# One block of products with ones per attention group: softmax sums gathered by a third adding transfer in rotating buffers, with loads, division and copies moved in their orders

## The chip, the cores and the metric

The kernel runs on one core of a Trainium2 chip. The metric is the device time of one execution in microseconds (us), lower is better. Engines are named as in the profile: PE (TensorE), DVE (VectorE), ACT (ScalarE), POOL (GpSimd), SP (SyncE, which only issues transfers here).

## The reference

A gated cross-attention block on x (2 x 512 x 1024) with a context (2 x 1024 x 1024): a quantised product with the context, a LoRA layer, a grouped-query attention, and a mixture of experts. Each is scaled by a gate and added to x. The part that the change touches is the attention:

```python
q = (query @ Wq).reshape(b, sq, NUM_HEADS, HEAD_DIM).transpose(0, 2, 1, 3)      # 32 heads of 32
k = (key @ Wk).reshape(b, sk, NUM_KV_HEADS, HEAD_DIM).transpose(0, 2, 1, 3)     # 8 heads of 32
v = (value @ Wv).reshape(b, sk, NUM_KV_HEADS, HEAD_DIM).transpose(0, 2, 1, 3)
k = jnp.repeat(k, rep, axis=1); v = jnp.repeat(v, rep, axis=1)                  # rep = 4
scores = jnp.einsum('bhqd,bhkd->bhqk', q, k) * scale
probs = jax.nn.softmax(scores, axis=-1)
out = jnp.einsum('bhqk,bhkd->bhqd', probs, v)
```

with 512 queries and 1024 keys in each of two batches.

## The kernel before

Every engine runs a list of instructions written out by hand; semaphores join them. The attention is 16 groups (`GROUPS`: 2 batches x 8 key heads). A group is the four query heads of one key head, in 32 steps (`STEPS`): step t = 4*kt + h takes block kt of 128 keys and head h. The loop is `group(g)` on PE and `exp_group(g)` on ACT.

In a step PE issues one product for the maxima of a group that comes 52 steps later (`score_step`, bf16, 512 columns; DVE reduces it in `maximum`), and one transposed product of scores (L1046), which ACT turns into exponentials (L1401) in a ring of four probability tiles `PB`, each 128 x 2048 fp32 (four heads of 512 queries). Every four steps, in `weigh`, PE multiplies a finished tile by the values: four fp32 products of 32 columns of weights each that stand side by side in the array (one block). At step 16 the next group's maxima are turned (`max_rows`), DVE and SP bring them as rows to the keys and queries (`rows_in`), and PE waits for these at the next group's step 0.

The softmax sums over 1024 keys are gathered on POOL. For pair j of a group (tiles 2j and 2j+1, four pairs) POOL adds two tiles into a buffer (L668); ACT may reuse the two tiles only when that is done (`p_add`). The buffers are `PS[0]` and `PS[1]` (halves of R[4]) and `PS[2]` (`stage_pair`). Pairs 0 and 2 go into `PS[0]` and `PS[2]`, pairs 1 and 3 both into `PS[1]`; after each of the latter POOL starts an adding transfer (L671, 1 MB, SBUF to SBUF) of `PS[1]` onto `PS[0]` or `PS[2]`. PE multiplies both results by ones (`total(g, j)`, another block of four fp32 products each, summed over partitions into bank 6), at steps 2 and 18 of the next group (`TOTAL_AT`). ACT copies the sums out at step 20 (`SUM_OUT_AT`).

The reciprocals go a long way: SP spreads the sums over partitions (`sums_in`, four loads), DVE inverts at step 8 (`FEW_AT`, `invert_few`), SP writes 8 KB to memory and reads it back as broadcasts (`reciprocals_in`), POOL multiplies (`divide`, behind pair 1), ACT makes the upper half at step 28 (`O_HI_AT`, `divided_hi`) and POOL the lower (`divided_lo`, behind pair 2), all for the group before the last.

SP's order in group g is: rows of the maxima, sums of g-2, then (from the end of group g-1 on) queries and keys of g+2, then the reciprocals. PE needs these queries and keys at step 12 of group g. POOL's order in group g is: pair 0, the copy of the next values (`stage_values`), pair 1, transfer, division of g-2, pair 2, lower part, pair 3, transfer.

After the last step PE runs the output products (L1003) of one tile, the two blocks with ones of the last group, and the other tiles, of which the first products already stand in the last groups' steps.

## Time and profile before

| what | value |
|---|---|
| median of 3 runs | 1241.37 us (1240.68 to 1242.19) |
| the profiled execution | 1243.45 us, its span 1241.6 us |
| granted PE clock | 0.994 of full speed |
| attention stage in the span | 424 to 822 us |
| adding transfers | 32 of 1 MB |
| blocks with values / with ones | 128 / 32 |

The span is the time between the first and the last instruction of the profile; durations below are from this one execution. L668 is line 668 of the kernel. PE's matmuls are pipelined, so the distance between two beginnings says more than the length of one. A block of four products is shown as x8, since each fp32 product has two records. "[0.77 <-DMA stage_pair<-R]" is idle time of the engine before the instruction and what ended it.

### The profile page before, as it was taken

The numbers are of one execution on the slowest core, as the hardware profiler recorded it, in microseconds if no ns is written. First come the engines' busy times: TensorE is split into PE (matmuls) and PEld (weight loads), VectorE is DVE, ScalarE is ACT, GpSimd is POOL, SyncE is SP. The second block draws the span as 40 slices with busy tenths as digits, with TensorE's granted clock in tenths as the row PEclk, the third lists the DMA queues.
The fourth block names the chain that finished last, engine by engine and source line by source line (L and its number), as shares of the span: only waits on it lengthen the run. The fifth ranks groups of instructions, "written<-read, shape, count | busy, mean of one in ns | idle before, by whom it ended". The sixth has DMA issues, their size and how long they took to land.

```text
span 1241.6 us, 16902 instructions
## 1 busy us (share of the span) xinstructions
PE 1215.0 (98%) x6440; PEld 511.5 (41%) x6440; DVE 784.4 (63%) x1375; ACT 475.2 (38%) x829; POOL 685.1 (55%) x300
## 2 busy tenths in 40 slices
PE   8998899999999999999999999999999999999998
PEld 6664444444444332222323223234444444444443
DVE  8997731433546788887878788135659846737622
ACT  4676321000100377776777677743252010010000
POOL 6006996600072188988999899870175543535510
PEclk9999899999999999999999999999999999999999
DMA  9577242411361146564655455443374442523301
GB/s 353 176 252 187 68 126 79 102 35 35 62 207 60 35 92 129 114 131 105 129 118 126 108 120 110 99 90 60 101 215 138 132 136 102 176 79 103 118 17 51
DMA packets 94301, 145.11 MB, mean 117 GB/s; under 512 B 54672, under 2 KB 64912, under 8 KB 90128
## 3 DMA queue, kind: packets, MB, share of 16 engines
q1 hardware_dynamic: 59712, 99.51, 26.0%
q0 software_dynamic: 4608, 33.56, 13.5%
q10 hardware_dynamic: 29904, 11.02, 4.0%
q8 instruction: 48, 0.79, 0.2%
q14 instruction: 29, 0.24, 0.1%
HBM read 89.16 MB, written 10.60 MB: 80 GB/s over the span
## 4 chain that ended last, share of the span: by engine, by line
PE 54%; POOL 19%; DMA 14%; DVE 9%; issue 3%; ACT 1%; SPq 0%; POOLq 0%; ACTq 0%; DVEq 0%
PE bank L702 47%; POOL R L668 12%; DMA stage_pair<-R 9%; DMA R<-R 4%; PE bank L1003 4%; POOL stage_pair L668 4%; DVE R L1502 1%; POOL xn L650 1%; POOL R L690 1%; PE bank L958 1%; DVE R L1549 1%; DVE stats L1515 1%; DVE xn L1542 1%; DVE XTl L1549 1%; POOL XTl L655 1%
## 5 line engine op out<-in xcount | busy, mean ns | idle before, releaser
L1774 DVE TENSOR_REDUCE mxp<-bank 128x1 f32<-128x512 f32 x512 | 323.2, 683 | 87.0 <-PE bank L958 85.1
L1401 ACT ACTIVATE R<-bank 128x512 f32<-128x512 f32 x512 | 271.8, 602 | 108.7 <-PE bank L1046 102.8
L702 PE MATMUL bank<-XTh,R 128*128 128x512 bf16 x896 | 278.5, 379 | 2.7 <-POOL R L690 1.5
L668 POOL TENSOR_TENSOR R<-R 128x2048 f32<-128x2048 f32 x48 | 222.3, 4632 | 79.2 <-ACT R L1401 51.0
L702 PE MATMUL bank<-R 128*128 128x512 bf16 x960 | 209.2, 379 | 0.0
L702 PE MATMUL bank<-XTl,R 128*128 128x512 bf16 x448 | 169.6, 379 | 0.0
L690 POOL TENSOR_TENSOR R<-stage_pair,R 128x1024 bf16<-128x1024 f32 x32 | 76.5, 2403 | 129.6 <-DVE R L1932 69.1
L702 PEld LDWEIGHTS bank<-R 128*128 128x128 bf16 x960 | 94.0, 98 | 113.2
L971 PE MATMUL bank<-R,stage_c 128*32 128x512 f32 x1024 | 136.4, 604 | 0.5 <-ACT R L1401 0.5
L1046 PE MATMUL bank<-R 98*128 98x512 bf16 x352 | 133.9, 381 | 0.9 <-DVE R L1802 0.8
L958 PE MATMUL bank<-R 96*128 96x512 bf16 x352 | 134.4, 382 | 0.0
L702 PEld LDWEIGHTS bank<-XTh,R 128*128 128x128 bf16 x896 | 87.5, 98 | 105.9 <-POOL R L690 2.1
L690 POOL TENSOR_TENSOR R<-stage_c,R 128x1024 bf16<-128x1024 f32 x32 | 76.3, 2396 | 59.1 <-DVE R L1932 50.2
L1474 ACT ACTIVATE R<-bank,b1t 128x512 f32<-128x512 f32 x32 | 22.0, 686 | 201.9 <-PE bank L702 201.9
L573 POOL TENSOR_TENSOR R<-stage_pair,zero 128x1024 f32 (+1 forms) x35 | 67.2, 1921 | 37.7 <-DMA stage_pair<-wts_in 26.2
L575 POOL TENSOR_TENSOR R<-stage_pair,R 128x1024 f32 (+1 forms) x35 | 75.9, 2167 | 5.9 <-POOL R L573 5.3
L668 POOL TENSOR_TENSOR stage_pair<-R 128x2048 f32<-128x2048 f32 x16 | 76.5, 4783 | 0.9 <-ACT R L1401 0.8
L958 PEld LDWEIGHTS bank<-R 96*128 96x128 bf16 x352 | 34.2, 97 | 98.5 <-DVE mxp L1774 64.4
L1003 PE MATMUL bank<-R,XTh 128*128 128x512 bf16 x256 | 70.5, 379 | 0.8 <-issue 0.8
L1981 DVE SCALAR_TENSOR_TENSOR X<-xn,TV,X 128x512 f32<-128x512 f32 x32 | 67.4, 2146 | 0.1
L1199 ACT ACTIVATE lnv<-lnv 128x1 f32<-128x1 f32 x32 | 6.4, 201 | 156.8 <-DVE lnv L1522 156.8
L1962 DVE CAST R<-R 128x512 bf16<-128x512 f32 x32 | 21.3, 667 | 70.5 <-ACT R L1474 70.5
(201 smaller groups left out, 1504.8 us busy)
## 6 DMA issues: line engine op xcount, KB each, us to landing
stage_pair<-wts_in SPq DMA_DIRECT2D x35, 512.0 KB, 3.5
R<-R POOLq DMA_DIRECT2D x16, 1024.0 KB, 7.6
stage_pair<-R POOLq DMA_DIRECT2D x16, 1024.0 KB, 7.0
stage_pair<-w_in SPq DMA_DIRECT2D x32, 512.0 KB, 3.6
stage_c<-w_in SPq DMA_DIRECT2D x32, 512.0 KB, 3.6
R<-q_scr SPq DMA_DIRECT2D x48, 128.0 KB, 2.6
XTh<-ctx_t_in SPq DMA_DIRECT2D x11, 512.0 KB, 6.9
XTh<-ctx_nat_in SPq DMA_DIRECT2D x9, 512.0 KB, 3.6
```

Of the source, the lines that this page charges most:

```text
L573: pool.tensor_tensor(hi, stage_w[stage][:, :], zero[:, :].to_broadcast([P, D]), ALU.add).then_inc(wt_hi, 1)
L575: pool.tensor_tensor(lo, stage_w[stage][:, :], hi, ALU.subtract).then_inc(wt_done, 1)
L668: pool.tensor_tensor(PS[(0, 1, 2, 1)[j]], PB[2 * j % 4], PB[2 * j % 4 + 1], ALU.add).then_inc(p_add, 1)
L690: pool.tensor_tensor(lo[:, cols], stage_e[(n - N_WT) % RING_E][:, :], hi[:, cols], ALU.subtract).then_inc(wt_done, 1)
L702: mm = pe.matmul(o, a, m, start=first and a is ah and bs is bh, stop=last and a is al)
L958: pe.matmul(bank[s_bank(u)][:, :], QS[g % 3][0:96, h * S + qt * P:h * S + (qt + 1) * P], KS[g % 3][0:96, kh * HALF:(kh + 1) * HALF], start ...
L971: mm = pe.matmul(out_bank[h * HD:(h + 1) * HD, :], weights, probs[:, h * S:(h + 1) * S], start=first, stop=last)
L1003: mm = pe.matmul(outs[h], a[i][:, cols], b[i][:, k * D + h * HALF:k * D + (h + 1) * HALF], start=k == 0 and i == 0, stop=k == KT - 1 and i ...
L1046: pe.matmul(bank[t_bank(g, t)][:, :], KS[g % 3][0:98, kt * P:(kt + 1) * P], QS[g % 3][0:98, h * S:(h + 1) * S], start=True, stop=True).the ...
L1401: act.activation(PB[kt % 4][:, h * S:(h + 1) * S], bank[t_bank(g, t)][:, :], ACT.Exp, scale=float(HD) ** -0.5).then_inc(exp_done, 1)
L1774: dve.tensor_reduce(mxp[head // REP % 2][:, m, n // 2, n % 2:n % 2 + 1], bank[s_bank(u)][:, :], AX.X, ALU.max).then_inc(s_max, 1)
L1981: dve.scalar_tensor_tensor(out=xh, in0=b2b[:, hc], scalar=TV[:, j * TT + t:j * TT + t + 1], in1=xh, op0=ALU.mult, op1=ALU.add).then_inc(eo ...
```

## The change

The sums of a group are now gathered into one buffer. Pair 0 is added straight into `total_in(g)`: `PS[0]` in even groups; in odd ones a part of XTh that is not yet in use (groups 1, 3, 5, 7; it has 8 pieces of 256 fp32 a partition, not adjacent), or the first half of V (groups 9 to 15). Pairs 1 to 3 go through `PS[1]` and `PS[2]`, whose roles change with the group's parity, and three adding transfers, here called B, C and D, bring them onto `total_in(g)` one after the other: B behind pair 1, C ahead of pair 3, and D behind pair 0 of the next group. The last group has two only: C is left out, D adds pair 3 onto pair 2, and PE makes two blocks. All views are in pieces of 256.

PE makes one block with ones a group, at step 30 of the next; ACT copies the sums at step 31. DVE inverts at step 14. The division stands behind pair 2, and the upper half (now at step 4) and the lower half (behind pair 1) are made one group later than before. SP loads queries and keys ahead of the sums. A scratch area of the experts' stage moves within V.

```diff
-TOTAL_AT = (2, 18)
-SUM_OUT_AT = 20
-FEW_AT = 8
+TOTAL_AT = 30
+SUM_OUT_AT = 31
+FEW_AT = 14
...
-O_HI_AT = 28
+O_HI_AT = 4
...
+        xth_1 = per_tile(XTh[:, :].bitcast(F32))[:, :, B * S // 4:B * S // 2]
...
+        def pieces(v):
+            return v.rearrange("p (k n) -> p k n", k=KT)
+        def total_in(g):
+            if g % 2 == 0:
+                return pieces(PS[0])
+            return xth_1 if g < KV_HEADS else pieces(V[:, 0:REP * S])
+        def beside(g, i):
+            return pieces(PS[1 + (g + i) % 2])
...
             for g in range(1, GROUPS):
                 rows_in(g)
-                if g >= 2:
-                    sums_in(g - 2)
                 if g + 2 < GROUPS:
                     sp.wait_ge(st_mm, STEPS * g)
                     queries_in(g + 2)
                     keys_in(g + 2)
+                if g >= 2:
+                    sums_in(g - 2)
                 if g >= 2:
                     reciprocals_in(g - 2)
...
+            def add_pair(g, j):
+                pool.wait_ge(exp_done, STEPS * g + 2 * REP * (j + 1))
+                if j == 0:
+                    if g >= 2:
+                        pool.wait_ge(one_mm, g - 1)
+                    dst = total_in(g)
+                elif j == 1:
+                    if g > 0:
+                        pool.wait_ge(ps_c, 16 * g)
+                    dst = beside(g, 0)
+                elif j == 2:
+                    if g > 0:
+                        pool.wait_ge(ps_d, 16 * g)
+                    dst = beside(g, 1)
+                else:
+                    pool.wait_ge(ps_b, 16 * (g + 1))
+                    dst = beside(g, 0)
+                pool.tensor_tensor(dst, pieces(PB[2 * j % 4]), pieces(PB[2 * j % 4 + 1]), ALU.add).then_inc(p_add, 1)
...
                 for j in range(KT // 2):
-                    pool.wait_ge(exp_done, STEPS * g + 2 * REP * (j + 1))
                     if j == 3:
-                        pool.wait_ge(ps_sum[0], 16 * (g + 1))
-                    elif g > 0 and j == 1:
-                        pool.wait_ge(ps_sum[1], 16 * g)
-                    elif g > 0:
-                        pool.wait_ge(one_mm, 2 * (g - 1) + j // 2 + 1)
-                    pool.tensor_tensor(PS[(0, 1, 2, 1)[j]], PB[2 * j % 4], PB[2 * j % 4 + 1], ALU.add).then_inc(p_add, 1)
-                    if j % 2 == 1:
-                        pool.wait_ge(p_add, 4 * g + j + 1)
-                        pool.dma_start(PS[j - 1], PS[1], accum_op=ALU.add).then_inc(ps_sum[j // 2], 16)
+                        pool.wait_ge(p_add, 4 * g + 3)
+                        pool.wait_ge(ps_b, 16 * (g + 1))
+                        if g + 1 < GROUPS:
+                            pool.dma_start(total_in(g), beside(g, 1), accum_op=ALU.add).then_inc(ps_c, 16)
+                    add_pair(g, j)
+                    if j == 0 and g > 0:
+                        pool.wait_ge(p_add, 4 * g)
+                        pool.wait_ge(ps_c, 16 * g)
+                        pool.dma_start(total_in(g - 1), beside(g - 1, 0), accum_op=ALU.add).then_inc(ps_d, 16)
+                    if j == 1:
+                        pool.wait_ge(p_add, 4 * g + 2)
+                        pool.dma_start(total_in(g), beside(g, 0), accum_op=ALU.add).then_inc(ps_b, 16)
+                    if j == 3 and g + 1 == GROUPS:
+                        pool.wait_ge(p_add, 4 * GROUPS)
+                        pool.dma_start(beside(g, 1), beside(g, 0), accum_op=ALU.add).then_inc(ps_d, 16)
                     if j == 0 and 1 <= g < GROUPS - 1:
                         stage_values(g + 1)
-                    if g >= 2 and j == 1:
+                    if g >= 3 and j == 1:
+                        divided_lo(g - 3)
+                    if g >= 2 and j == 2:
                         divide(g - 2)
-                    if g >= 2 and j == 2:
-                        divided_lo(g - 2)
...
+            def over_pieces(weights, probs, first, last):
+                n = KT // REP
+                for h in range(REP):
+                    mm = pe.matmul(bank[6][h * HD:(h + 1) * HD, :].rearrange("p (k n) -> p k n", k=n), weights,
+                                   probs[:, h * n:(h + 1) * n, :], start=first, stop=last)
+                return mm
...
-            def total(g, j):
-                pe.wait_ge(ps_sum[j], 16 * (g + 1))
-                if j == 0 and g > 0:
+            def total(g):
+                if g > 0:
                     pe.wait_ge(sum_out, g)
-                over_keys(bank[6], onesf[:, 0:HD], PS[2 * j], j == 0, j == 1).then_inc(one_mm, 1)
+                if g + 1 < GROUPS:
+                    pe.wait_ge(ps_d, 16 * (g + 1))
+                    over_pieces(onesf[:, 0:HD], total_in(g), True, True).then_inc(one_mm, 1)
+                else:
+                    pe.wait_ge(ps_b, 16 * GROUPS)
+                    over_pieces(onesf[:, 0:HD], total_in(g), True, False)
+                    pe.wait_ge(ps_d, 16 * GROUPS)
+                    over_pieces(onesf[:, 0:HD], beside(g, 1), False, True).then_inc(one_mm, 1)
...
-                    if g > 1 and t == O_HI_AT:
-                        divided_hi(g - 2)
+                    if g > 2 and t == O_HI_AT:
+                        divided_hi(g - 3)
```

## Rows read from the trace of the kernel before

**Rows 1.** The page, busy us, share of the span and instructions of each engine

```profile
PE 1215.0 (98%) x6440; PEld 511.5 (41%) x6440; DVE 784.4 (63%) x1375; ACT 475.2 (38%) x829; POOL 685.1 (55%) x300
```

**Rows 2.** Timeline (start us, us, instruction), PE's fp32 blocks, 603 to 614 us

```profile
603.55 1.06 PE L971 MATMUL bank<-R,stage_c 128*32 128x512 f32 x8
...
606.40 1.06 PE L971 MATMUL bank<-R,stage_c 128*32 128x512 f32 x8
...
609.50 1.07 PE L971 MATMUL bank<-R,stage_c 128*32 128x512 f32 x8
...
610.38 1.04 PE L971 MATMUL bank<-stage_pair,onesf 128*32 128x512 f32 x8
...
613.20 1.07 PE L971 MATMUL bank<-R,stage_c 128*32 128x512 f32 x8
```

**Rows 3.** Timeline, PE's blocks around the first and last of six waits

```profile
558.72 1.07 PE L971 MATMUL bank<-R,stage_c 128*32 128x512 f32 x8
...
560.55 1.06 PE L971 MATMUL bank<-stage_pair,onesf 128*32 128x512 f32 x8 [0.77 <-DMA stage_pair<-R]
...
563.40 1.06 PE L971 MATMUL bank<-R,stage_c 128*32 128x512 f32 x8
...
796.91 1.06 PE L971 MATMUL bank<-R,stage_c 128*32 128x512 f32 x8
...
799.16 1.07 PE L971 MATMUL bank<-R,onesf 128*32 128x512 f32 x8 [1.18 <-DMA R<-R]
...
802.03 1.06 PE L971 MATMUL bank<-R,stage_c 128*32 128x512 f32 x8
```

**Rows 4.** Timeline, POOL, one group (L668 adds, L671 transfers)

```profile
598.02 4.53 POOL L668 TENSOR_TENSOR R<-R 128x2048 f32<-128x2048 f32 x1 [0.21 <-ACT R L1401]
602.84 0.87 POOL L671 DMA_DIRECT2D stage_pair<-R  x1 [0.30 <-POOL R L668]
603.45 4.83 POOL L668 TENSOR_TENSOR R<-R 128x2048 f32<-128x2048 f32 x1
607.93 0.69 POOL L636 COPY stage_c<-V 128x256 f32<-128x256 f32 x1
610.09 4.53 POOL L668 TENSOR_TENSOR R<-R 128x2048 f32<-128x2048 f32 x1 [1.48 <-DMA stage_pair<-R]
614.93 0.87 POOL L671 DMA_DIRECT2D R<-R  x1 [0.30 <-POOL R L668]
615.53 1.58 POOL L650 TENSOR_TENSOR xn<-stage_c,xn 128x512 f32<-128x512 f32 x1
616.77 4.83 POOL L668 TENSOR_TENSOR stage_pair<-R 128x2048 f32<-128x2048 f32 x1
621.26 1.45 POOL L655 TENSOR_TENSOR XTl<-xn,XTh 128x512 bf16<-128x512 f32 x1
622.54 4.64 POOL L668 TENSOR_TENSOR R<-R 128x2048 f32<-128x2048 f32 x1
```

**Rows 5.** Timeline, ACT, the first exponentials of a group

```profile
596.81 1.58 ACT L1401 ACTIVATE R<-bank 128x512 f32<-128x512 f32 x3 [0.44 <-POOL stage_pair L668]
```

**Rows 6.** Landing times of one line's transfers: L671 (adding, 32), then L475 (14)

```profile
DMA to landing us min/median/max: 6.9/7.4/9.2
...
DMA to landing us min/median/max: 1.4/6.3/8.3
```

**Rows 7.** Busy time by window: PE, PEld, DVE, ACT, POOL, clock, DMA share, GB/s

```profile
385.00:423.00 38.00, 38.00 (x177) 16.95 (x175) 23.12 (x35) 4.24 (x8) 0.00 (x0) 1.00 0.13 42
616.00:620.40 4.40, 4.40 (x28) 1.29 (x28) 3.68 (x7) 3.48 (x7) 4.40 (x2) 1.00 1.04 208
```

**Rows 8.** Timeline, SP's issues: query loads, and the write of the reciprocals

```profile
595.76 1.56 SPq L452 DMA_DIRECT2D R<-q_scr  x3
...
603.61 0.34 SPq L475 DMA_DIRECT2D r_scr<-few  x1
```

**Rows 9.** Timeline, PE, the last block with ones

```profile
835.53 1.06 PE L971 MATMUL bank<-stage_pair,onesf 128*32 128x512 f32 x8 [0.75 <-DMA stage_pair<-R]
```

17 lines of the change are left out of this document (10 added, 7 removed).

## The prediction, made before the changed kernel was run

> **What bounds the kernel now.** I read the engines' totals first: TensorE (PE) is busy for 98% of the span [rows 1], so a change pays only in what it takes off PE's own order, or in what makes PE wait. The edited code runs in the attention stage alone (16 groups of 32 steps, from 424 to 822 us), so the next view is PE's timeline there, at the beginnings of the blocks of four fp32 products with the values (one block every four steps, in `weigh`). Between two plain blocks lie 2.85 us [rows 2]; the interval in which the maxima are turned takes 3.10, and an interval that also holds a block of products with ones takes 3.70. A group has five plain intervals, one with the turn and two with ones: 5 x 2.845 + 3.10 + 2 x 3.70 = 24.73 us. A block with ones therefore costs 3.70 - 2.84 = 0.86 us of PE.
>
> Measured over all 128 blocks, PE stands still for longer than this at six places, and only there; every one is a block with ones that waits for its adding transfer. The first takes 4.68 us instead of 3.70 (0.98), the last 5.12 (1.42) [rows 3]; the six together are 5.0 us. So PE is the bound, and the transfers of the sums are the one thing that breaks into it.
>
> Next comes POOL, since ACT may overwrite a pair of probability tiles only after POOL has added it. POOL and the transfers form a loop with little room: add j=3 at 598.02, transfer at 602.84, add j=1 released by it at 610.09, transfer at 614.93, and add j=3 again at 622.54 [rows 4]: 24.52 us against PE's 24.73. ACT already stands 0.44 us for POOL at a group's start [rows 5]. This closeness decides the forecast.
>
> **What PE saves.** In the loop two blocks with ones a group become one, in 15 groups: 15 x 0.86 = 12.9 us. After the loop the last group keeps two blocks. The new block reads its 512 columns as two pieces of 256; columns and passes are the same, so I take the same 0.86; bounds: 0 (nothing extra) and another 0.86 if pieces were to cost as much again, which would undo the saving. The lower end is nearer: blocks with values and with ones, of different buffers and weights, all take 1.04 to 1.07 us [rows 2], so that the count of columns seems to set the price.
>
> **The six stalls.** The sum is now wanted at step 30 of the next group, about 19.3 us after that group's start. Its third transfer starts behind add j=0, at about 10.3, and lands at about 17.5. So PE has some 2 us in hand where it had none, and the 5.0 us go. The profiled execution took 1243.45 us (1241.6 of span, 1.85 around it), 2.08 over the median of the runs, so it may hold more of such stalls than a usual run: on the median I count 4.
>
> Without anything new the sum is 1241.4 - 12.9 - 4.0 = 1224.5 us.
>
> **What the change adds: POOL.** A group of PE would take 24.73 - 0.86 = 23.87 us. POOL's work, back to back, from [rows 4]: four adds of 4.49 (616.77 to 621.26) = 17.96; one gap of 0.30 between an add and the transfer that needs it (only behind j=1; behind j=2 the division fills it); three issues of 0.60 instead of two = 1.80; copy of values 0.69; division 1.24; its lower part 1.28. That is 23.27 us, 0.60 under PE. It fits, barely; an add dearer by 0.15 us through its pieces would use all of it. I take nothing for the pieces, and keep 0 to 0.3 us an add: 0 to 7 us in all.
>
> **What it adds: transfers.** I set up one group, with time from the last exponential of the group before (596.37 in the group shown, where ACT's wait of 0.44 began [rows 5]). Add j=0 starts when exponential 8 is done, 5.8, ends 10.3; D (the third transfer of the group before) starts there. Copy; j=1 from 11.75 to 16.3; B starts at 16.6. Lower part of the division; j=2 from 18.4 to 22.9; division to 24.1, which is 0.2 into the next group; there C starts, if B has landed; j=3 from 0.8 to 5.3; then j=0 again at 5.8. A transfer lands 6.9 at best, 7.4 in the median and 9.2 us at worst after its start [rows 6]. B: 16.6 + 7.4 = 24.0, wanted at 24.1. C: 0.2 + 7.4 = 7.6, wanted at 10.3. D: 17.7, wanted at 18.4. So B has 0.1 us of its own and D 0.7, plus the 0.45 us that POOL idles; C has 2.7. A late B holds C and j=3 in POOL's order, and behind them j=0 and the copy; a late D holds j=2, the division and C; for j=2 ACT's first exponential of the next group waits, and so PE. In before, 5 transfers of 32 land after more than 8 us; with 48 of them, two thirds in tight places, I expect five such hits of 0.5 to 1.5 us on PE: about 4 us.
>
> The transfers keep the DMA engines busy while they last: share 1.04 at 208 GB/s between 616.0 and 620.4 [rows 7], so 1.05 MB take 5.0 us of all 16. Three a group are 15 of 23.9 us, where two of 24.7 were 10. What meets one waits for its end: the 8 KB write of the reciprocals, issued 0.77 us behind a transfer [rows 4, 8], lands in 6.3 us in the median, and in 1.4 with none in flight [rows 6].
>
> The page "DMA: Bandwidth & Descriptors" of the Trainium skill (section "Issuing engines are not separate DMA queues") says that DMAs of different issuers interleave on the 16 engines. If that held finely, the write of 8 small pieces an engine would not last nearly as long as the whole transfer; the trace says otherwise. By the page the queue of SP could be left out of the sum, which would then be 1 us lower; by the trace it has to be followed.
>
> **What is moved past what.** SP now issues three query and three key loads at the group's start and the four loads of sums behind them. The first loads go at -0.6 (595.76, when PE had finished the group's last product) and the queries take SP 1.56 us [rows 8], all six some 3.7. C starts at 0.2, so the later half may lie under it until 7.3, and the keys land at about 8.1; PE wants them at step 12, at 7.7. Cost 0 to 0.4 us a group, 13 times; since a stall there gives POOL room and C an earlier start, I take 0.1: about 1 us. The loads of sums land by 8.5; VectorE wants them at step 14, 9.8: hidden. The write of the reciprocals went at 7.24 for step 8 [rows 8]; without the block with ones at step 2, and with six steps and one more block with values, 3.7 us, it goes at 10.1, just ahead of D at 10.3, and lands by 12.5; the four broadcast loads and the two loads of maxima rows lie under D until 18, wanted at 22.9 (division) and 23.3 (next group's first product): hidden, by 5 us, as long as the write comes first.
>
> ScalarE's copies of the sums (now at step 31) and of the divided output (now at step 4) are as many as before, and ScalarE is busy for 38% of the span [rows 1]; nothing. The extra half microsecond of POOL's issue is counted above. After the last exponential the path is as before: add j=3, one transfer, one block with ones (835.53) [rows 9]; the inversions of group 14 move behind the loop on VectorE, 3.4 us, under a PE tile of 10 us.
>
> **Pieces of 1 KB.** In groups 1, 3, 5 and 7 the destination is cut into 8 pieces a partition, so 12 transfers of 48 consist of 1 KB pieces instead of 8 KB. Bounds: as fast as now, or each piece dearer by what a plain 1 KB piece takes. Between 385 and 423 us nearly only 1 KB pieces move: 42 GB/s at share 0.13 [rows 7], 20 GB/s an engine, 51 ns a piece. 64 pieces an engine at 51 ns more are 3.3 us a transfer: landing at 10.7. I take the lower third, +0.5 to 1 us, since 20 GB/s an engine is no poor rate beside the 12.5 that adding transfers reach with 8 KB. By the timetable +1 us costs little over 2 us in all.
>
> Stalls of the new form: 4 (late transfers, pieces among them) + 1 (keys) = 5. **Forecast: 1224.5 + 5 = 1229.5 us.**
>
> **Rivals.**
> A. Everything is hidden: 1224.5, or 1223.5 if all 5.0 us go. For it: 0.60 us of room on POOL. Against it: B's 0.1 us.
> B. POOL and transfers set the pace at 24.4 to 24.7 us a group (adds dearer by 0.3 us, or B at 8 us each time): 0.5 to 0.8 us x 15 = 8 to 12 us over A: 1233 to 1237. For it: landings of 7.5 to 7.9 are frequent.
> C. Slower, by the pieces: in an odd group the chain j=1, B, C must fit between exponential 16 and the next group's add j=0; it does up to a landing of 8.2 us. Each us beyond costs once at j=3 and once at j=2 of the group behind, by 8 groups about 10 us a us. At 10.7: 25 us over the forecast, 1254; slower than before from a landing of 9.5. Against it: 20 GB/s. The page named above ("Why small descriptors are slow (HBM only)") says that transfers within SBUF do not suffer from small pieces; no row shows an adding one in 1 KB pieces.
> D. Slower or even, by the order of D and the write of reciprocals. They are 0.2 us apart. If the write comes second, it lands with D at 17.4; broadcasts and maxima rows are issued from there to 20.3 and meet B, whose data move from 17.5 to 23.5; the next group's first product, wanted at 23.3, waits to about 24.5: 1.2 us x 13 = 16 us: 1241 to 1246.
> E. The block with ones costs twice as much in pieces, or the change saves PE nothing: about 1241.
>
> **How the numbers follow.** Chances: forecast (1225.5 to 1233) 0.45, A 0.20, B 0.15, C 0.08, D 0.10, E 0.02. Faster by over 0.2% (about what a measurement of this kernel can tell from none), below 1238.9: forecast, A, most of B, 0.77. Within: the end of B, part of D, E: 0.10. Slower: C and half of D, 0.13. The range goes from A's lower edge, 1222.5, to 1243, and leaves out C, D's upper half and a little below.
>
> **What would show it.** Right: 16 blocks with ones in the loop and its end, two in the last group; blocks with values 2.85 us apart, 3.71 once a group; no PE idle released by the adding transfers at step 30; a period near 24.0. Late B or D: ACT's idle time released by POOL's add j=2, POOL's by the transfer ahead of j=2 or j=3. Rival C: landings over 9 us in groups 1, 3, 5, 7 and long periods only up to group 8. Rival D: landing of the 8 KB write near 6.5 us and PE waiting for the rows at step 0. Rival B: adds over 4.6 us or a period of 24.4 in every group. The forecast is wrong if PE's idle time grows over 12 us.

## The result, and the profile after it

The changed kernel takes 1255.55 us in the median (1254.08 to 1258.0) against 1241.78 us for the kernel before on the same chip (1240.68 to 1244.32). The ratio is 1.0115, with a 95% interval from 1.0100 to 1.0131: it is slower by 1.15%. The forecast was 1229.5 us, its range ended at 1243.0, and "slower" had a chance of 0.13. The prediction was wrong in sign, and the time lies outside its range.

These are the first lines of the page of the changed kernel (span; busy time and share of each engine), the line of POOL's DMA queue (packets, MB, share of 16 engines) and the page's four lines on its adding transfers (count, size, median us from issue to landing; 40 of the 47, the other seven are XTh<-R x4 and V<-R x3):

```profile
span 1252.3 us, 16625 instructions
PE 1203.8 (96%) x6238; PEld 507.4 (41%) x6320; DVE 786.9 (63%) x1375; ACT 474.3 (38%) x829; POOL 706.1 (56%) x315
q0 software_dynamic: 17520, 49.29, 21.7%
R<-R POOLq DMA_DIRECT2D x16, 1024.0 KB, 7.9
R<-stage_pair POOLq DMA_DIRECT2D x9, 1024.0 KB, 7.7
XTh<-stage_pair POOLq DMA_DIRECT2D x8, 1024.0 KB, 9.8
V<-stage_pair POOLq DMA_DIRECT2D x7, 1024.0 KB, 7.8
```

PE's busy time did fall, from 1215.0 [rows 1] to 1203.8 us, and its share fell too, from 98% to 96%: it now waits. (82 of PE's products are missing from this trace, 49 of them of line 745, outside the attention stage, so that the busy time reads a few us low; inside the stage idle time was counted separately, below.) The twelve transfers into XTh, which consist of 1 KB pieces, land in 8.9 to 10.5 us, the other 35 in 7.8 us in the median.

What PE was to save, it saved. In group 10 of the changed kernel the blocks with values start at these times (the block with ones lies between 701.80 and 705.50):

```profile
693.26 1.07 PE L1014 MATMUL bank<-R,stage_c 128*32 128x512 f32 x8
696.10 1.06 PE L1014 MATMUL bank<-R,stage_c 128*32 128x512 f32 x8
698.95 1.06 PE L1014 MATMUL bank<-R,stage_c 128*32 128x512 f32 x8
701.80 1.07 PE L1014 MATMUL bank<-R,stage_c 128*32 128x512 f32 x8
705.50 1.07 PE L1014 MATMUL bank<-R,stage_c 128*32 128x512 f32 x8
708.37 1.06 PE L1014 MATMUL bank<-R,stage_c 128*32 128x512 f32 x8
```

Plain intervals are 2.84 and 2.85 us, and the single one with ones is 3.70, as it was in [rows 2]. The one group in which nothing waits (12, counted from 0) lasts 23.91 us; 23.87 was expected. But of the 14 groups 1 to 14 only two come below 24 us, and the worst are group 3 with 29.2 and group 13 with 30.1.

**Where the time went.** I cut 424 to 850 us into windows of 1 us (view by stretch) and summed two things over them: PE's idle time, and its busy time at the lower clock, of which half is lost. The changed kernel has 23.7 us of idle time where the kernel before has 6.2, and loses 6.6 us to the clock where the kernel before loses nothing. 17.5 + 6.6 - 12.9 saved = 11.2 us; the two spans differ by 1252.3 - 1241.6 = 10.7 us, so these two account for it to within 0.5 us. The idle time has three kinds.

*First, an exponential waits for POOL's add of the last pair, which was late because the transfer ahead of it was.* Timeline of the changed kernel (start, duration, engine, line, operation, and in brackets the idle time before it and what ended it), POOL, then ACT and PE's weight loads, groups 1 and 2. The bracket of a weight load is the idle time of the loads; PE's products stand for 0.3 to 0.9 us less. A stall of PE, below, is that of its products, unless weight loads are named:

```profile
471.01 1.55 POOL L702 DMA_DIRECT2D XTh<-R  x1 [3.89 <-DMA XTh<-stage_pair]
471.98 5.15 POOL L694 TENSOR_TENSOR stage_pair<-R 128x2048 f32<-128x2048 f32 x1
476.47 5.12 POOL L694 TENSOR_TENSOR R<-R 128x2048 f32<-128x2048 f32 x1
480.93 2.17 POOL L707 DMA_DIRECT2D XTh<-stage_pair  x1
477.24 3.54 ACT L1457 ACTIVATE R<-bank 128x512 f32<-128x512 f32 x7 [2.96 <-POOL stage_pair L694]
477.88 0.10 PEld L1103 LDWEIGHTS bank<-R,stage_c 98*128 98x128 bf16 x1 [1.91 <-ACT R L1457]
```

POOL stands 3.89 us for transfer B, which was issued at 460.96 and landed 9.5 us later. Its add of pair 3 then starts at 471.98 and is recorded to 477.13, the exponential that waits for it starts at 477.24, and PE's products have stood for 1.6 us (its weight loads for 1.91). This kind is found in groups 2 to 8 above all, those that have or follow a transfer of 1 KB pieces, and makes up most of what PE loses there: intervals of 4.8, 6.6, 5.0, 5.1 and 5.7 us instead of 2.85 in groups 2, 3, 4, 6 and 8.

*Second, the keys of a coming group land late* (group 11; groups 1, 10 and 13 have the same, and their intervals are 5.0 us too long in the four):

```profile
714.18 0.10 PEld L1001 LDWEIGHTS bank<-R 96*128 96x128 bf16 x1 [1.85 <-DMA R<-k_scr]
```

*Third, the write of the reciprocals leaves behind transfer D instead of ahead of it* (groups 11 and 13; here first group 3, where it does no harm, then group 13: SP's queue, POOL, PE):

```profile
507.79 1.16 POOL L707 DMA_DIRECT2D R<-R  x1
508.09 0.34 SPq L492 DMA_DIRECT2D r_scr<-few  x1
765.76 0.88 POOL L707 DMA_DIRECT2D R<-R  x1
766.79 0.34 SPq L492 DMA_DIRECT2D r_scr<-few  x1
773.70 2.49 SPq L495 DMA_DIRECT2D xn<-r_scr  x4
777.57 1.41 SPq L476 DMA_DIRECT2D R<-row_l  x1
773.33 0.87 POOL L710 DMA_DIRECT2D V<-stage_pair  x1 [0.78 <-POOL stage_pair L694]
783.07 1.26 POOL L667 TENSOR_TENSOR xn<-stage_c,xn 128x512 f32<-128x512 f32 x1 [3.19 <-DMA xn<-r_scr]
783.32 0.39 PE L1103 MATMUL bank<-R,stage_c 98*128 98x512 bf16 x1 [3.29 <-DMA R<-row_l]
```

The write is issued 1.03 us after D and lands 6.9 us later, at 773.7; the broadcasts and the maxima rows behind it then meet transfer B of 773.33 and land at 783, 3.3 us late. Being second is not enough for this: the write was also issued 0.28 to 0.43 us behind D in groups 3 (the first two lines), 10 and 12, and landed in 1.4 us there, as it did up to group 14 wherever it was ahead. Over this kernel, e1_whole and e4_whole_few12, writes up to 0.53 us behind D land in 1.4 us, and the six that are 0.55 us or more behind in 5.8 to 7.4 us.

The second and third kind hang together. All six late writes stand in groups in which PE had waited for keys at step 12, by 0.7 to 1.4 us: the wait holds up the inversion at step 14 and with it the write, while D, which follows the exponentials of earlier steps, leaves in time. (In e4_whole_few12 the inversion stands at step 12 itself.)

**The clock.** At three of these stalls the granted clock fell. The view by stretch of the changed kernel, around the stall of 2.1 us that ends at 504.43 (stretch, us, PE busy, granted clock, DMA share, GB/s):

```profile
503.00:504.00 1.00, 0.00 (x0) 1.00 0.73 140
504.00:505.00 1.00, 0.57 (x2) 0.55 0.75 134
505.00:506.00 1.00, 1.00 (x4) 0.50 0.00 0
508.00:509.00 1.00, 1.00 (x8) 0.50 0.04 4
```

The clock falls at about 504.1, while PE still stands; PE runs at 1.2 GHz until about 510.9, and the block at 507.53 takes 1.94 us instead of 1.06. So group 3, with a stall of 2.1 us, took 5.3 us more than group 12 without one (29.19 against 23.91). The other two such stretches are at 534 to 538 and 784 to 788, behind stalls of 1.7 and 3.3 us; the stall of 2.5 us in group 8 (it ends at 638.35) was followed by none. The kernel before has no such stretch between 424 and 850 us. The clock also goes with the scatter between executions of one kernel: those of v3_lead16 below range from 1233.4 us at a mean granted clock of 1.000 to 1242.6 us at 0.992.

### The profile page after: what moved, and what is told of

It reads as the page before. It is cut to its first block, busy times and chain, and to the rows that moved or that the text cites. A ratio compares the mean times of both kernels' runs of the same rounds, so it can differ in the third digit from the quotient of the medians.

```text
span 1252.3 us, 16625 instructions
## 1 busy us (share of the span) xinstructions
PE 1203.8 (96%) x6238; PEld 507.4 (41%) x6320; DVE 786.9 (63%) x1375; ACT 474.3 (38%) x829; POOL 706.1 (56%) x315
## 3 DMA queue, kind: packets, MB, share of 16 engines
q1 hardware_dynamic: 59712, 99.51, 25.6%
## 4 chain that ended last, share of the span: by engine, by line
PE 59%; DMA 13%; POOL 11%; DVE 9%; issue 4%; ACT 1%; SPq 1%; POOLq 0%; DVEq 0%; ACTq 0%
PE bank L745 46%; DMA XTh<-stage_pair 6%; POOL stage_pair L694 5%; PE bank L1060 4%; POOL R L694 3%; PE bank L1001 3%; PE bank L1014 2%; PE bank L1103 2%; DMA R<-k_scr 2%; DVE R L1559 1%; DMA R<-R 1%; POOL R L733 1%; DMA r_scr<-few 1%; DVE R L1606 1%; DVE stats L1572 1%
## 5 line engine op out<-in xcount | busy, mean ns | idle before, releaser
L745 PE MATMUL bank<-XTh,R 128*128 128x512 bf16 x877 | 273.8, 379 | 3.6 <-POOL R L733 1.5
L694 POOL TENSOR_TENSOR R<-R 128x2048 f32<-128x2048 f32 x32 | 156.9, 4905 | 50.1 <-ACT R L1457 49.2
L745 PE MATMUL bank<-XTl,R 128*128 128x512 bf16 x437 | 165.5, 379 | 0.6
L1014 PE MATMUL bank<-R,stage_c 128*32 128x512 f32 x1024 | 139.0, 615 | 1.2 <-ACT stage_c L1436 0.7
L694 POOL TENSOR_TENSOR stage_pair<-R 128x2048 f32<-128x2048 f32 x24 | 114.8, 4785 | 9.0 <-ACT R L1457 5.8
L590 POOL TENSOR_TENSOR R<-stage_pair,zero 128x1024 f32 (+1 forms) x35 | 67.2, 1920 | 36.2 <-DMA stage_pair<-wts_in 25.6
L1103 PE MATMUL bank<-R,stage_c 98*128 98x512 bf16 x160 | 60.9, 384 | 8.3 <-ACT R L1457 5.0
L653 POOL COPY stage_c<-V 128x256 f32<-128x256 f32 x16 | 16.1, 1008 | 89.6 <-PE bank L745 89.6
```

What stands on the lines that cost most here:

```text
L590: pool.tensor_tensor(hi, stage_w[stage][:, :], zero[:, :].to_broadcast([P, D]), ALU.add).then_inc(wt_hi, 1)
L694: pool.tensor_tensor(dst, pieces(PB[2 * j % 4]), pieces(PB[2 * j % 4 + 1]), ALU.add).then_inc(p_add, 1)
L745: mm = pe.matmul(o, a, m, start=first and a is ah and bs is bh, stop=last and a is al)
L1014: mm = pe.matmul(out_bank[h * HD:(h + 1) * HD, :], weights, probs[:, h * S:(h + 1) * S], start=first, stop=last)
L1103: pe.matmul(bank[t_bank(g, t)][:, :], KS[g % 3][0:98, kt * P:(kt + 1) * P], QS[g % 3][0:98, h * S:(h + 1) * S], start=True, stop=True).the ...
```

## The experiments

Theory P: the 1 KB pieces make 12 of the 47 adding transfers late, and POOL's order hands it on. Theory S: SP's small loads (keys, rows, reciprocals) wait out whichever adding transfer they meet. Theory L: POOL and its transfers form a loop without slack, so that any relief of PE only meets the loop. All times are medians, each beside runs of the kernel before on the same chip. Differences between two experiments, each of 4 to 12 executions, are uncertain by some 2 to 4 us (an estimate from the intervals of the ratios), and traces are of one execution each: that of e1_whole took 6.1 us more than its median, that of v3_lead16 4.7, of e8_sums_first 4.3, of v5_few13 2.9, the others at most 2.1 us more or less.

**e1_whole: the pieces taken away.** Groups 1, 3, 5 and 7 gather over the last two tiles of X, 8 KB a partition in one piece (the residual of these tiles is lost in the output).

```diff
-            return xth_1 if g < KV_HEADS else pieces(V[:, 0:REP * S])
+            return pieces(X[:, 6 * D:8 * D] if g < KV_HEADS else V[:, 0:REP * S])
```

> The changed kernel, but in groups 1, 3, 5 and 7 the sums are gathered in 8 KB of X that lie together instead of the 8 pieces of 1 KB in XTh (this spoils a part of x; nothing else is left out). Theory P (the pieces, with landings of 9.2 to 10.5 us, cause most of the 31 us of new stalls): the 19 us of stalls in groups 2 to 8 shrink to under 5, the landings come to 7.0 to 8.0, and the time to 1237 to 1243 us. Theory T (the third transfer as such, pieces or not, overloads POOL's order and the DMA engines): little over 4 us come back, 1250 to 1256 us, and groups 2 to 8 look as groups 9 to 13 of the changed kernel.

Measured: 1242.37 us, ratio 1.0020 (0.9997 to 1.0042). Against 1255.55 the pieces cost 13 us (12 if each is taken against its own runs of the kernel before). The time is in theory P's range and far from T's. In the traced execution (1248.45 us, among the slowest of ten) the long intervals of groups 4, 6 and 8 are gone; waits of the weight loads for keys (1.1 to 1.9 us in five groups) and for rows (groups 2, 11 and 13) are left. Two parts of P's expectation missed there: groups 2 to 8 are still 11.4 us over 23.91 each, not under 5, and the 8 KB landings in them reach from 7.0 to 10.2 us, not 8.0. P holds, and it is 13 of the 31 us by which the changed kernel lies over 1224.5, the time with everything hidden.

**e6_before_pieces: the pieces alone, in the kernel before.** Two transfers a group as before; only the first pair's destination in groups 1, 3, 5 and 7 is the low tiles of X's transposed copy. (Adds and blocks with ones go over pieces of 256 columns everywhere, as in the changed kernel; a block with ones still takes 3.70 - 2.85 us.)

```diff
+            def first(g):
+                return xth_1 if g % 2 == 1 and g < KV_HEADS else pieces(PS[0])
...
-                        pool.dma_start(PS[j - 1], PS[1], accum_op=ALU.add).then_inc(ps_sum[j // 2], 16)
+                        pool.dma_start(first(g) if j == 1 else pieces(PS[2]), pieces(PS[1]), accum_op=ALU.add).then_inc(ps_sum[j // 2], 16)
```

> The kernel BEFORE (two adding transfers and two blocks with ones a group), with one part of the change alone: in groups 1, 3, 5 and 7 the first pair of sums gathers in the low tiles of X's transposed copy, so the destination of one adding transfer of the group is cut in eight pieces of 1 KB a partition. 4 transfers of 32 are so cut. Theory P (a transfer of 1 KB pieces lands 2 to 2.5 us later, whatever stands around it): these four land in 9 to 10 us against 7.4 of the others; each of them is wanted at the next block with ones, so PE waits 1.5 to 2.5 us in each of the four groups: 6 to 10 us, 1247 to 1251. Rival (they land late in the changed kernel only because three transfers a group crowd one another): 7.4 to 8 us, 1241 to 1243.

Measured: 1248.83 us, ratio 1.0074 (1.0049 to 1.0099). The four landed in 9.7, 9.8, 9.7 and 9.5 us, the other 28 in 6.9 to 9.1 with a median of 7.2. The view of the line that issues them (count, ns min/median/max, first and last start), and one of the waits:

```profile
L678 POOL DMA_DIRECT2D R<-R x12: 862/867/994, 437.6 to 821.8; - x12
L678 POOL DMA_DIRECT2D XTh<-R x4: 1580/1584/1590, 461.7 to 620.3; - x4
575.82 0.16 PEld L1000 LDWEIGHTS bank<-XTh,onesf 128*32 128x32 f32 x8 [3.10 <-DMA XTh<-R]
```

So the price of the pieces, +2.3 us of landing against the 7.4 of [rows 6], does not need three transfers a group; POOL takes 0.7 us longer over the instruction, and between 515.2 and 520.2 us, with such a transfer under way, the DMA engines move 171 GB/s at share 1.20, where [rows 7] have 208 at 1.04. PE lost 1.0, 1.8, 4.0 and 1.3 us in the four groups; the third again drew a stretch at 1.2 GHz (3.4 us).

**e2_small_d: the third transfer cut to an eighth.** D adds one of its eight pieces (most of pair 3 is missing from the sums; 1 is added so that they have a reciprocal). Pieces in XTh stay in B and C.

```diff
-                        pool.dma_start(total_in(g - 1), beside(g - 1, 0), accum_op=ALU.add).then_inc(ps_d, 16)
+                        pool.dma_start(total_in(g - 1)[:, 0:1, :], beside(g - 1, 0)[:, 0:1, :], accum_op=ALU.add).then_inc(ps_d, 16)
```

> The changed kernel with the transfer behind pair 0 (D) cut to an eighth (one piece of eight, so a part of the sums lacks pair 3; 1 is added to all sums against zeros). B and C stay whole, with their pieces. Theory T (the third transfer's load): the excess goes, 1226 to 1232 us. Theory P (the pieces): B and C of groups 1, 3, 5 and 7 still land after 9 us or more and still hold pair 3, so only about a third of the stalls goes: 1240 to 1247 us.

Measured: 1244.74 us, ratio 1.0043 (1.0023 to 1.0064), 11 us under the changed kernel. No wait for rows is left, so that D was what held the write; late adds in groups 2, 4, 6 and 8 (2 to 3.6 us) and late keys stay, so that B and C have their own share. The time is in the range of theory P (1240 to 1247), not of T. Even with D nearly gone the kernel is no faster than before.

**e3_one_block: PE relieved, the transfers left alone.** The kernel before with one block with ones a group; a product of 16 columns takes the place of the other (its half of the sums is left out, 1 is added).

```diff
+                if j == 0 and g + 1 < GROUPS:
+                    pe.matmul(bank[6][0:HD, 0:16], onesf[:, 0:HD], PS[0][:, 0:16], start=True, stop=True).then_inc(one_mm, 1)
+                    return
```

> The kernel before with one block of products with ones a group instead of two (the first is replaced by one product of 16 columns, so the sums lack pairs 0 and 1; 1 is added to all sums against zeros); transfers, POOL and SP unchanged. If PE alone sets the pace, 15 blocks of 0.86 us go: 1229 us, or 1226 with some of the stalls. If POOL's loop with its two transfers (24.52 us as measured) binds behind PE, a group can't be shorter than that, and only 15 x 0.2 = 3 us go: 1236 to 1239 us.

Measured: 1249.83 us, ratio 1.0082 (1.0058 to 1.0105). With less work for PE the kernel became *slower*, and both forecasts (1226 to 1229, 1236 to 1239) missed; nine groups last 25.0 to 25.7 us where 24.77 was the rule. SP's queue and POOL of this kernel, in group 5 and then in group 8:

```profile
549.11 0.34 SPq L475 DMA_DIRECT2D r_scr<-few  x1
549.15 0.87 POOL L671 DMA_DIRECT2D stage_pair<-R  x1 [0.30 <-POOL R L668]
557.02 4.53 POOL L668 TENSOR_TENSOR R<-R 128x2048 f32<-128x2048 f32 x1 [2.11 <-DMA stage_pair<-R]
626.85 0.88 POOL L671 DMA_DIRECT2D stage_pair<-R  x1 [0.30 <-POOL R L668]
628.02 0.34 SPq L475 DMA_DIRECT2D r_scr<-few  x1
R<-R POOLq DMA_DIRECT2D x16, 1024.0 KB, 7.5
stage_pair<-R POOLq DMA_DIRECT2D x16, 1024.0 KB, 7.7
```

The write of the reciprocals and the transfer now start at the same moment, and the `stage_pair` transfers land in 7.7 us in the median where they took 7.0 in the kernel before; POOL waits for them, then ACT, then PE. In group 5 the write lands in 1.4 us, so that the broadcasts behind it are read while the transfer runs. In two groups no broadcast can: 1, which has no write, and 8, where the write is again 1.2 us behind and lands in 6.0. There the transfer lands in 6.9 and 7.0 us and the group lasts 23.93 us: PE's saving was had. That the broadcasts are what makes the other landings longer is read from the trace and was not tried by itself. What the run does show is L's core, with a condition: the loop of POOL and transfers was already the second limit, at 25.3 us a group with landings of 7.7; in the two groups with 7.0 it did not bind.

**e4_whole_few12: the order of write and D.** As e1_whole, and VectorE's inversion of the few reciprocals, with SP's write behind it, at step 12 (the line `FEW_AT = 14` becomes `FEW_AT = 12`).

> As e1_whole, and VectorE inverts the sums at step 12 instead of 14, so that the 8 KB write of the reciprocals goes 0.9 us earlier and well ahead of transfer D. If the order of this write and D costs time (rival D: 6 us in two groups of the changed kernel), it is 3 to 8 us faster than e1_whole and no write lands after 6 us; if the loads of the sums are not in by step 12, VectorE waits for them and it is slower by up to 10 us. If neither, it is equal to e1_whole.

Measured: 1238.40 us, ratio 0.9985 (0.9966 to 1.0004), 4.0 us under e1_whole; the two intervals overlap a little, so that the size of this step is loose. In the traced executions PE's waits for rows fell from three groups to one (its interval 1.7 us too long, the write 0.55 us behind D and landing in 7.4, against the expectation that none would land after 6), and no stretch at 1.2 GHz is left. A wait for keys and the one for rows:

```profile
504.61 0.10 PEld L1001 LDWEIGHTS bank<-stage_c,R 96*128 96x128 bf16 x1 [1.79 <-DMA stage_c<-k_scr]
697.41 0.10 PEld L1103 LDWEIGHTS bank<-R,stage_c 98*128 98x128 bf16 x1 [2.04 <-DMA R<-row_l]
```

**e5_keys_later: the keys.** As e4_whole_few12, with `LEAD = 18` instead of 20.

> The changed kernel with contiguous sums (groups 1, 3, 5, 7 gather over two tiles of X, so the residual of these two tiles in the output is lost) and the few reciprocals at step 12, as in the run before (1238.40), and one number more: LEAD 18 instead of 20, so that the first score product that needs a group's new keys comes two steps (1.4 us) later. Theory K (the keys that SP loads at the group's start lie under the second adding transfer and cost PE about 1 us in each of 7 or 8 groups): waits of the score product's weight load for k_scr go, 6 to 8 us, to 1231 to 1233. Theory L (the wait for keys only takes up time that PE would then spend waiting for ScalarE behind POOL's adds, since POOL and transfers set the pace at about 24.8 us a group): the waits for keys go, the periods stay near 24.8 to 25, 1237 to 1239.

Measured: 1230.72 us, ratio 0.9927 (0.9901 to 0.9954), 7.7 us under e4_whole_few12. Theory S for the keys holds at its full price and theory L falls as the *remaining* limit: the two groups without any late DMA (8 and 9) last 23.91 us, and the others from 1 to 13 24.0 to 25.6. What was not run is `LEAD = 18` alone, with the inversion still at step 14: since every late write stood behind a wait for keys, it might have given part of the 4.0 us of the step before as well.

**e8_sums_first: SP's old order.** The changed kernel, with the four loads of sums ahead of queries and keys.

```diff
+                if g >= 2:
+                    sums_in(g - 2)
                 if g + 2 < GROUPS:
                     sp.wait_ge(st_mm, STEPS * g)
                     queries_in(g + 2)
                     keys_in(g + 2)
-                if g >= 2:
-                    sums_in(g - 2)
```

> The changed kernel with one part undone: SP issues the four loads of the sums ahead of the next group's queries and keys again, as the kernel before does. Theory K (keys are late because they lie under the second adding transfer, which goes out some 0.8 us behind SP's first load): the keys leave 2.4 us later, all of them under that transfer, and behind it they land as late as before or up to 1 us later; PE then waits for keys in nearly every group from 1 to 13, 1 to 2 us each: 1260 to 1275 against 1255.5. Rival (what leaves ahead of the transfer or behind it lands together when it ends, so the order makes no difference): 1253 to 1258.

Measured: 1297.42 us, ratio 1.0449 (1.0403 to 1.0495), above even theory K's range. Transfer C, SP's keys, and the weight load that needs them:

```profile
470.77 1.55 POOL L702 DMA_DIRECT2D XTh<-R  x1 [3.51 <-DMA XTh<-stage_pair]
475.73 3.53 SPq L463 DMA_DIRECT2D R<-k_scr  x3
481.87 0.10 PEld L1001 LDWEIGHTS bank<-R 96*128 96x128 bf16 x1 [4.13 <-DMA R<-k_scr]
480.00:482.00 2.00, 0.13 (x1) 0.50 0.46 147
482.00:484.00 2.00, 2.00 (x6) 0.50 0.08 12
```

The keys leave 5 us behind C and land when it has landed. PE's products stand 3.8 us in this group, and the granted clock (fourth number of the last two lines) is 0.50 behind the stall; every group from 2 to 13 now has an interval of 6.7 to 9.9 us and one of 3.7 to 4.9 behind it. The change of SP's order that the changed kernel brings is therefore needed, and it is worth 42 us there. In the windows of 1 us this kernel has 46.5 us of idle time and 32.1 lost at 1.2 GHz, against 23.7 and 6.6: my expectation of 5 to 20 us was short of the idle time by a little and had no term for the clock, which is over half.

**e9_two_numbers: both numbers, with the pieces.** The changed kernel with `FEW_AT = 12` and `LEAD = 18`, nothing else.

> The changed kernel with its 1 KB pieces, and two numbers changed: few reciprocals at step 12 instead of 14, and LEAD 18 instead of 20. Theory of three separate costs (pieces 13 us, keys 7 us, rows and reciprocals' order 4 to 6 us): the last two go, 1255.5 - 12 = 1242 to 1245. Theory of overlap (a late add behind a transfer of pieces and a late key fall on the same groups and hide one another): only 3 to 6 us go, 1249 to 1252.

Measured: 1247.03 us, ratio 1.0048 (1.0030 to 1.0067). 8.5 us go, between the two theories: separate costs would give 12, overlapping ones 3 to 6.

**v3_lead18: the whole result with contiguous sums.** As e5_keys_later, but the two tiles of X are written to DRAM in the queries' stage and loaded back in four quarters in groups 10 to 13.

```diff
+                if item == 9:
+                    sp.wait_ge(x_up, 4 * TT)
+                    sp.dma_start(x_scr, X[:, 6 * D:8 * D]).then_inc(x_save, 16)
...
+                    sp.dma_start(X[:, 6 * D + back.start:6 * D + back.stop], x_scr[:, back]).then_inc(x_back, 16)
```

> The changed kernel, whole result: contiguous sums for groups 1, 3, 5 and 7 over two tiles of X that are written to DRAM in the queries' stage and loaded back in groups 10 to 13; few reciprocals at step 12; new keys wanted two steps later (LEAD 18). It differs from the run of 1307.6 us in one thing, the subtraction for the divided output's lower part, which stays on POOL. Theory V (in that run VectorE's subtraction, two operands of SBUF, took 4.84 us because it stood beside POOL's add of 4.5 us and VectorE's maxima came late, some 6 us in each of 12 groups): without it 1230 to 1234, at most 3 us over the 1230.7 of the run that lost the two tiles of X, since only the four loads back are added. Rival (the loads back of 0.5 MB cost several us each beside the adding transfers): 1236 to 1242, with the long periods in groups 10 to 13.

Measured: 1232.44 us, ratio 0.9933 (0.9917 to 0.9948). It is faster than the kernel before by 0.67% and than the changed kernel by 1.8%. Against e9_two_numbers it shows the pieces once more: 14.6 us. Its median is 1.7 us over e5_keys_later's, within the noise, so that the loads back cost little.

**v2_all: POOL's subtraction moved to VectorE.** As v3_lead18, with one thing more.

```diff
-                    if g >= 3 and j == 1:
-                        divided_lo(g - 3)
+                    if g > 2 and t == DLO_AT:
+                        dve.wait_ge(o_hi, g - 2)
+                        dve.tensor_tensor(XTl[:, o_cols(g - 3)], onat, XTh[:, o_cols(g - 3)], ALU.subtract).then_inc(o_lo, 1)
```

> The changed kernel with the 1 KB pieces taken away without giving up any of the result: in groups 1, 3, 5 and 7 the sums gather in the two last tiles of X as one piece of 8 KB a partition; those tiles are written to DRAM in the queries' stage and loaded back in four quarters in groups 10 to 13. Besides, the reciprocals of the few heads (VectorE's inversion and with it SP's 8 KB write) come at step 12 instead of 14, ahead of the third adding transfer; the first product that needs the new keys comes 2 steps later; and the subtraction that gives the divided output's lower part (1.28 us of POOL a group) moves to VectorE at step 8. Theory P+S (pieces, and small loads that wait out an adding transfer, are what the change costs; POOL's lack of room is the rest): the run with contiguous sums and step 12 took 1238.40; keys 2 steps later give back about 1 us in 8 groups, POOL's room the few stalls by its add j=3, about 3 us: 1227 to 1231, faster than the kernel before (1240.8) by 1%. Theory L (POOL and transfers as a loop set the pace at about 24.8 us a group, whatever the small loads do): the loop has no wait for the lower part any more, so 1232 to 1236. If the four loads back of 0.5 MB collide with the adding transfers: up to 4 x 2 us more.

Measured: 1307.62 us, ratio 1.0548 (1.0523 to 1.0573): 75 us over v3_lead18, a clear miss. Eight of VectorE's subtractions (busy us, mean ns), and one of them beside POOL, with PE's weight load and the clock behind it:

```profile
L1882 DVE TENSOR_TENSOR XTl<-xn,XTh 128x512 bf16<-128x512 f32 x8 | 38.7, 4836 | 0.0
558.62 4.51 POOL L708 TENSOR_TENSOR X<-R 128x2048 f32<-128x2048 f32 x1 [0.52 <-ACT R L1469]
558.85 4.84 DVE L1882 TENSOR_TENSOR XTl<-xn,XTh 128x512 bf16<-128x512 f32 x1
564.34 0.10 PEld L1013 LDWEIGHTS bank<-R 96*128 96x128 bf16 x1 [4.17 <-DVE mxp L1843]
564.00:566.00 2.00, 1.66 (x4) 0.50 0.98 197
```

What took POOL 1.28 us [rows 4] takes VectorE 4.84, since it starts 0.23 us behind an add of POOL and ends 0.56 behind that add's end. VectorE's maxima stand behind it, PE's products stand 3.7 us for them (its weight loads 4.17), and then run at 1.2 GHz: in most groups one interval is 5.1 us too long and the next up to 1.7. The Trainium skill, page "SBUF — State Buffer" (section "Terms"), says that VectorE and GpSimd share one pair of ports, held exclusively for a whole instruction; by that rule the move was wrong from the start, and this trace agrees.

**v3_lead16 and v5_few13: one step further each way.** v3_lead18 with `LEAD = 16`, and v3_lead18 with `FEW_AT = 13`.

> As the run beside it, with LEAD 16: the new keys wanted another two steps (1.4 us) later, and the maxima two steps nearer to their use. In the run of 1230.7 us waits for keys of 0.6 to 1.1 us were left in groups 1, 2 and 12, and longer intervals without an own stall beside them, some 3 us in all. Theory K: these go, 2 to 3 us less than the run beside it. Rival (the stalls left belong to POOL's last add of a group and to late sums, not to the keys): no difference, within 1 us; if the maxima come too late for their rows, slower.

Measured: 1237.86 us, ratio 0.9965 (0.9951 to 0.9979), 5.4 us over v3_lead18. In the traced execution, the slowest of twelve, no wait for keys of note is left, but PE now waits for the maxima at their turn, 0.37 us or more in each group, and most when VectorE has stood for late sums at step 12 (1.7 to 2.0 us in groups 10 to 12: PE loses 1.8 to 2.4 us there), and three stretches at 1.2 GHz follow (5.1 us). The rival of late maxima holds; theory K's 2 to 3 us less does not.

> The whole-result version of 1232.44 us with one number changed: the few reciprocals at step 13 instead of 12. In that version VectorE stands at step 12 for the loads of the sums in nearly every group, by 1.6 us in groups 10 and 11, where PE loses 1.2 us each. Theory T (the sums land just after step 12, and the write of the reciprocals, 0.7 us later, still leaves before the third adding transfer): these stalls go, 2 to 4 us less, 1228.5 to 1230.5. Rival D (0.7 us are enough to put the write behind the third transfer in some groups, so that the maxima rows land late): one to three groups lose 1 to 4 us each at the next group's first product, 1232 to 1238.

Measured: 1233.25 us, ratio 0.9920 (0.9905 to 0.9936): the same as v3_lead18. PE's loss behind late sums shrank as theory T has it (from 1.2 to 0.5 us in group 10), and rival D's came in their place: PE waits for maxima rows in groups 10, 11 and 13, 0.5 to 0.7 us each. Of the steps tried, 12, 13 and 14, none is free of both.

**The account over all kernels**, from the same windows of 1 us between 424 and 850 us (idle: PE's idle us; clock: us lost at 1.2 GHz; last column: idle and clock less those of the kernel before, less 12.9 where the second block with ones is gone):

| kernel | idle | clock | span | span less before's | account |
|---|---|---|---|---|---|
| before | 6.2 | 0 | 1241.6 | | |
| after | 23.7 | 6.6 | 1252.3 | +10.7 | +11.2 |
| e1_whole | 19.3 | 4.5 | 1246.6 | +5.0 | +4.7 |
| e3_one_block | 20.2 | 3.2 | 1246.8 | +5.2 | +4.3 |
| e4_whole_few12 | 14.7 | 0 | 1238.3 | -3.3 | -4.4 |
| e5_keys_later | 7.0 | 0 | 1227.1 | -14.5 | -12.1 |
| e6_before_pieces | 11.7 | 3.4 | 1247.5 | +5.9 | +8.9 |
| e9_two_numbers | 16.9 | 6.7 | 1244.7 | +3.1 | +4.5 |
| v3_lead18 | 7.7 | 0 | 1229.9 | -11.7 | -11.4 |
| v3_lead16 | 14.4 | 5.1 | 1240.8 | -0.8 | +0.4 |
| v5_few13 | 9.8 | 0 | 1234.3 | -7.3 | -9.3 |

It closes to within 3 us (for e2_small_d, not shown, it is 4.8 off), so the attention stage's own waits and their clock account for the differences to that grain; steps smaller than this can't be read from it. The spans are those of the traced executions: by medians e1_whole is only 1.5 us over the kernel before.

## Why the prediction was wrong, point by point

- **What PE saves, 12.9 us: right.** 0.86 us a block, the read in two pieces of 256 at no extra cost, a floor of 23.91 against 23.87.
- **The six stalls, 5.0 us: right in kind.** No block with ones waits for an adding transfer at step 30 by more than 0.2 us; the two long intervals there are rows.
- **POOL's sum, 23.27 us: right for groups with 8 KB pieces, wrong with 1 KB pieces.** Issues of pieces take POOL 0.93 to 0.97 us to the next instruction instead of 0.60. The adds themselves start 4.49 us apart (471.98 and 476.47) as before, so that the term I feared was nothing and the one I left out was 0.35 us an issue.
- **Pieces of 1 KB, taken at +0.5 to 1 us: mis-sized, and the largest error.** They land in 8.9 to 10.5 us, +2.3 at e6's clean comparison. The bound of 10.7 from the plain 1 KB pieces [rows 7] held and should have had the weight; that 20 GB/s "is no poor rate beside the 12.5" compared plain pieces with adding ones, and no row showed the two together. What rival C cites from the Trainium skill (page "DMA: Bandwidth & Descriptors", section "Why small descriptors are slow (HBM only)"), that transfers within SBUF do not suffer from small pieces, does not hold for these adding ones: 9.7 us against 7.4. Rival C had the mechanism, the groups and the slope: (9.7 - 8.2) x 10 = 15 us against 13 to 15 measured. It had a chance of 0.08. (The sum took 48 transfers; with two in the last group they are 47.)
- **Keys, 0.1 us a group: mis-sized.** The timetable had them at 8.1 for 7.7. In the changed kernel four groups lose 5.0 us by them; in e4_whole_few12 the weight loads wait 1.1 to 1.8 us for them in seven groups, and e4 against e5 gives 7.7 us in all, 0.6 a group. I had argued the computed 0 to 0.4 down to 0.1 because "a stall there gives POOL room"; it didn't.
- **Order of D and the write (rival D, 0.10): half right.** 0.2 us between them was too close for one outcome: the write came second in five groups of the changed kernel, but only in the two where it was over 1 us behind did the chain run as described; these cost 6.2 us (e1 to e4: 4.0). What put it so far behind was the wait for keys at step 12, a link that the prediction did not have: it took keys and order for separate.
- **Late transfers, five hits of 0.5 to 1.5 us: too few.** 8 KB transfers land in 7.8 us in the median and up to 10.2 where [rows 6] had 7.4 and 9.2. I put this down to three a group and the small loads between them; no run separates the two. With B's 0.1 us in hand, half a microsecond is a hit in nearly every group. In v3_lead18 something of this remains: 24.3 to 25.4 us a group from 1 to 13, but for group 9 with 23.91.
- **The clock: a term that was not there.** Each long stall was counted at its own length. 6.6 us of the 31 were the clock behind three stalls. [Rows 3] had only stalls up to 1.4 us, with nothing behind them; that no longer one was to be seen was a reason to ask for a price, and not for zero.

The step that failed is therefore the stalls of the new form, taken at 5 us in all: the medians give 6.2 for what is left in e5_keys_later (1230.7 - 1224.5, late transfers above all), 7.7 for keys, 4.0 for the order and 13.2 for the pieces, 31 us together, the clock's share inside them. This chain ends at 1255.6 because it is made of differences of the same medians, and is no check. A check is e9_two_numbers: with the pieces in place keys and order give back 8.5 us, not 11.7, so the terms seem to overlap by some 3 us, which is near the noise. The chances were wrong as well as the centre: three terms, all on the side of slower, had each been set by an argument below the middle of its bounds.

## What to carry to other kernels

When a change removes work from the bound engine but adds transfers that others wait for, set up the timetable first and believe its margins: a margin of 0.1 to 0.4 us against landings that scatter by 2 us is a cost in most rounds, not a small one. Cost a stall of the matrix engine of some 2 us at between its own length and twice that and more, since the clock may fall at it (the group with 2.1 us of waiting lost 5.3 here, one with 2.0 us in group 6 lost no clock). And keep the destination of a frequent transfer contiguous: 1 MB saved to DRAM and loaded back once was cheaper by 14.6 us than twelve transfers in small pieces.

## What the runs showed of the hardware that was not expected

- An adding transfer of 1 MB within SBUF lands in 6.9 to 7.6 us in most cases with 8 KB a partition in one piece (23 of 32 in the kernel before), and in 9.5 to 9.8 with eight pieces of 1 KB (e6_before_pieces); its issue takes POOL 1.58 instead of 0.87 us.
- A small DMA of another queue that leaves while such a transfer runs mostly lands when it does: the 8 KB write in 6.9 us against 1.4 alone, keys in e8_sums_first at 481.3 to 481.8 us behind a transfer that lands at 481.1. One that leaves in the first half microsecond after the transfer's issue still gets through: writes up to 0.53 us behind land in 1.4 us. The page "DMA: Bandwidth & Descriptors" of the Trainium skill (section "Issuing engines are not separate DMA queues") has the DMAs of different issuers interleave; at this grain these traces show a wait, and SP's queue had to be costed by the transfers.
- PE's granted clock went from 2.4 to 1.2 GHz at stalls of 1.7, 2.1 and 3.3 us and stayed there for 3.4 to 6.8 us, but kept 1.00 at one of 2.5 us; in e9_two_numbers it fell at stalls of 1.9, 2.2 and 2.4 us and not at two of 2.0 and 2.1. The length of the stall alone does not tell.
- VectorE's subtraction of two SBUF operands took 4.84 us beside POOL's add, where POOL itself needed 1.28.
- Less work for PE alone made the kernel slower by 0.8% (e3_one_block), with the landings of its `stage_pair` transfers 0.7 us longer.
